# Causal grouped attention: the softmax division by block transposes on VectorE in place of two TensorE turns

## The reference, cut to what matters

```python
q = _rope((x @ Wq.T + bq) by head);  k = _rope((x @ Wk.T + bk) by head);  v = x @ Wv.T + bv
k, v = each repeated for 4 query heads
att = einsum('bhqd,bhkd->bhqk', q, k) / sqrt(16)
att = where(causal, att, -inf)
att = softmax(att, axis=-1)
y = einsum('bhqt,bhtd->bhqd', att, v)
return y.transpose(0, 2, 1, 3).reshape(b, t, n) @ Wo.T + bo
```

## Time and profile before

| | |
|---|---|
| time, median of 3 runs | 1556.51 us (1552.51 to 1558.87) |
| the profiled execution's own time | 1555.63 us |
| its span, from first to last instruction | 1553.9 us |
| mean granted clock of TensorE | 0.984 |
| busy share of the span: PE, DVE, ACT, POOL | 92%, 62%, 49%, 36% |
| the stage: its first DMA issue to that of the next stage | 1068.87 to 1227.92 us |

### The profile page before, as it was taken

One profiled execution on the slowest core, in us unless ns is written; L12 is line 12 of the kernel. 1 busy time (PEld: TensorE's weight loads), 2 busy tenths in 40 slices (PEclk: granted clock), 3 DMA queues, 4 the chain that ended last, 5 costly groups with the idle time before them and its releaser, 6 DMA issues. The chain is left out here.

```text
span 1553.9 us, 29211 instructions
## 1 busy us (share of the span) xinstructions
PE 1437.0 (92%) x10604; PEld 1116.8 (72%) x10630; DVE 968.4 (62%) x2214; ACT 754.9 (49%) x1878; POOL 562.0 (36%) x556
## 2 busy tenths in 40 slices
PE   6999999999899989899999999999899898999897
PEld 4778777787689777777777766896555688733586
DVE  5766667666565674756566566648675563677663
ACT  5565656656245334344343443453454353489352
POOL 2835619354136345525234200472000165110173
PEclk9999999999999999999999999999999899999998
DMA  3122231212282342303112005526000343222534
GB/s 144 59 90 69 85 103 42 90 63 90 69 330 79 112 148 103 115 17 103 40 45 99 1 1 214 201 97 227 9 2 2 131 140 129 64 63 47 188 100 139
DMA packets 57454, 149.48 MB, mean 96 GB/s; under 512 B 10225, under 2 KB 24689, under 8 KB 57201
## 3 DMA queue, kind: packets, MB, share of 16 engines
q1 hardware_dynamic: 39664, 89.58, 16.8%
q0 software_dynamic: 17664, 58.21, 11.0%
HBM read 104.77 MB, written 38.27 MB: 92 GB/s over the span
## 5 line engine op out<-in xcount | busy, mean ns | idle before, releaser
L145 POOL TENSOR_SCALAR ln_var<-ln_moments 128x4 f32<-128x4 f32 x16 | 4.0, 252 | 392.3 <-DVE ln_moments L130 242.4
L1376 ACT ACTIVATE s_scratch<-s_bank,s_neg_max 128x128 f32<-128x128 f32 (+3 forms) x128 | 67.2, 527 | 108.7 <-DVE s_neg_max L1467 108.5
L412 POOL DMA_INDIRECT expert_rows<-s_y,s_to_row x92 | 91.2, 991 | 57.8 <-ACT s_y L736 36.7
L1467 DVE TENSOR_REDUCE s_neg_max<-s_bank 128x1 f32<-128x128 f32 (+3 forms) x128 | 59.5, 487 | 52.5 <-PE s_bank L1262 52.2
L2811 POOL TENSOR_TENSOR s_w_hi<-s_w_raw,zero 128x1024 fp32r<-128x1024 f32 x25 | 55.5, 2221 | 100.0 <-PE s_memory L81 77.1
L1260 PE MATMUL s_bank<-s_k,s_q 128*128 128x128 f32 (+3 forms) x256 | 89.8, 446 | 0.0
L953 DVE TENSOR_TENSOR s_h_e<-s_bank,s_silu_e 128x176 f32<-128x176 f32 x92 | 31.4, 341 | 83.7 <-ACT s_silu_e L724 79.7
L79 PE MATMUL s_bank<-xn_t_hi,s_w_hi 128*128 128x512 f32 x192 | 79.7, 415 | 1.2 <-DVE xn_t_lo L212 1.2
L2476 ACT ACTIVATE s_exps<-s_bank,s_rms 128x512 f32<-128x512 f32 x128 | 76.4, 696 | 3.9 <-PE s_bank L2367 3.9
L1477 DVE TENSOR_SCALAR s_scratch<-s_scratch,s_row_sum 128x128 f32<-128x128 f32 (+3 forms) x128 | 75.4, 589 | 4.5
L405 POOL DMA_INDIRECT s_xg<-normed_rows,s_from_row x64 | 63.9, 998 | 38.5 <-DVE s_from_row L848 20.2
(11 more groups left out here) (429 smaller groups left out, 4852.5 us busy)
## 6 DMA issues: line engine op xcount, KB each, us to landing
s_expert_w_lo<-experts_lo SPq DMA_DIRECT2D x32, 608.0 KB, 13.1
s_e_lo<-in_experts POOLq DMA_DIRECT2D x32, 304.0 KB, 3.1
experts_hi<-s_e_hi POOLq DMA_DIRECT2D x32, 304.0 KB, 2.5
experts_lo<-s_e_lo POOLq DMA_DIRECT2D x32, 304.0 KB, 2.9
s_expert_w_hi<-experts_hi SPq DMA_DIRECT2D x16, 608.0 KB, 12.2
s_w_raw<-in_wa_o SPq DMA_DIRECT2D x16, 512.0 KB, 3.5
s_yg<-expert_rows SPq DMA_DIRECT2D x32, 256.0 KB, 4.5
s_raw<-in_shared SPq DMA_DIRECT2D x16, 384.0 KB, 6.4
```

The source lines that it names most:

```text
L412: pool.indirect_dma_start(out=y_rows[:, :], out_offset=bass.IndirectOffsetOnAxis(ap=to_row[:, i:i + 1].bitcast(U32), axis=0), in_=y[:, i % ...
L1376: act.activation(probs[:, h % 2, r, 0:(r + 1) * P], score_bank(h, r), ACT.Exp, bias=neg_max[:, 4 * h + r:4 * h + r + 1], accum_out=row_sum ...
L1467: dve.tensor_reduce(neg_max[:, 4 * h + r:4 * h + r + 1], score_bank(h, r), AX.X, ALU.max, negate=True).then_inc(max_done, 1)
```

## The change

The two TensorE turns and their two places in the ring are taken out. In their place VectorE divides in the layout that `o_raw` has: a block transpose of `o_raw` puts the sums of a slot on that slot's partitions by query (`by_query`), 16 reciprocals are taken, a second block transpose, whose source repeats each reciprocal 32 times, spreads them over the slot's rows (`inverse`, now 128 x 512), and a multiplication of two SBUF tiles gives `o`. The first transpose (`scale_o`) stands between M2a and M2b, the other three (`scale_rest`) between M1a and M1b, `low_o` behind `split_shift`, and `rotate_q` directly behind M3b. ScalarE's `high_o` reads SBUF and stands behind the last exponentials of the unit. In unit 7 the attended values are read from PSUM, without `copy_o`, and the matmuls of zeros between its attention and the last projection become 20 (they were 5 and 6).

```diff
-        o_raw, inverse, o = sb("o_raw", [P, S]), sb("inverse", [P, TB, KV_HEADS]), sb("o", [P, S])
+        o_raw, inverse, o = sb("o_raw", [P, S]), sb("inverse", [P, S]), sb("o", [P, S])
+        by_query, by_query_inverse = sb("by_query", [P, S]), sb("by_query_inverse", [P, S // SLOT])
...
                     if x == 1:
-                        order += [("turn", U - 1)] * (U > 0) + [("q", U + 2)] * (U + 2 < UNITS)
-                    if x == 3:
-                        order += [("back", U - 1)] * (U > 0)
+                        order += [("q", U + 2)] * (U + 2 < UNITS)
...
-            return order + [("turn", UNITS - 1), ("back", UNITS - 1), ("out", len(OUTS) - 1)]
+            return order + [("out", len(OUTS) - 1)]
...
-                    if j == 0:
-                        if U:
-                            turn_o(U - 1)
-                        if U + 2 < UNITS:
-                            project_q(U + 2)
-                    if j == 1 and U:
-                        turn_o_back(U - 1)
+                    if j == 0 and U + 2 < UNITS:
+                        project_q(U + 2)
...
-            turn_o(UNITS - 1)
-            turn_o_back(UNITS - 1)
-            keep_busy(pe, res, held("back", UNITS - 1)[:, 1, :], 6)
+            keep_busy(pe, res, held("att", UNITS - 1)[:, 1, :], 20)
             project_out(len(OUTS) - 1)
-            keep_busy(pe, res, held("back", UNITS - 1)[:, 1, :], 9)
+            keep_busy(pe, res, held("att", UNITS - 1)[:, 1, :], 9)
...
             def copy_o(U):
                 act.wait_ge(attended, TB * (U + 1))
                 if U:
-                    act.wait_ge(o_natural, U)
+                    act.wait_ge(o_scaled, U)
                 act.activation(o_raw[:], single("att", U), ACT.Copy).then_inc(o_copied, 1)

             def high_o(U):
-                act.wait_ge(o_ready, U + 1)
+                act.wait_ge(o_scaled, U + 1)
...
-                act.activation(o_hi[:, U % 3, :], single("back", U), ACT.Copy).then_inc(o_hi_done, 1)
+                act.activation(o_hi[:, U % 3, :], o[:], ACT.Copy).then_inc(o_hi_done, 1)
...
-                    if j == 1 and U:
+                    if j == (3 if U + 1 < UNITS else 1) and U:
                         high_o(U - 1)
...
-            copy_o(UNITS - 1)
             high_o(UNITS - 1)
...
             def scale_o(U):
-                by_head = single("turn", U).rearrange("p (t g s) -> p t g s", t=TB, s=SLOT)
-                dve.wait_ge(o_natural, U + 1)
-                dve.reciprocal(inverse[:], by_head[:, :, :, HD]).then_inc(inverse_done, 1)
+                if U + 1 < UNITS:
+                    dve.wait_ge(o_copied, U + 1)
+                    attended_values = o_raw[:]
+                else:
+                    dve.wait_ge(attended, TB * UNITS)
+                    attended_values = single("att", U)
+                if U:
+                    dve.wait_ge(sums_inverted, U)
+                dve.transpose(by_query[:], attended_values).then_inc(sums_turned, 1)
+
+            def scale_rest(U):
+                attended_values = o_raw[:] if U + 1 < UNITS else single("att", U)
+                dve.wait_ge(sums_turned, U + 1)
+                if U:
+                    dve.wait_ge(inverse_done, U)
+                dve.reciprocal(by_query_inverse[:], by_query[:].rearrange("p (b r) -> p b r", r=SLOT)[:, :, HD]).then_inc(sums_inverted, 1)
+                dve.wait_ge(sums_inverted, U + 1)
+                if U:
+                    dve.wait_ge(o_scaled, U)
+                dve.transpose(inverse[:], by_query_inverse[:].unsqueeze(2).broadcast_to([P, S // SLOT, SLOT])).then_inc(inverse_done, 1)
                 dve.wait_ge(inverse_done, U + 1)
                 if U:
-                    dve.wait_ge(o_ready, U)
-                dve.tensor_tensor(o[:].rearrange("p (t g s) -> p (t g) s", t=TB, s=SLOT),
-                                  single("turn", U).rearrange("p (t g s) -> p (t g) s", t=TB, s=SLOT),
-                                  spread(inverse[:].rearrange("p t g -> p (t g)"), SLOT), ALU.mult).then_inc(o_scaled, 1)
+                    dve.wait_ge(o_lo_done, U)
+                dve.tensor_tensor(o[:], inverse[:], attended_values, ALU.mult).then_inc(o_scaled, 1)
...
-                dve.tensor_tensor(o_lo[:, U % 3, :], single("back", U), f32(o_hi[:, U % 3, :]), ALU.subtract).then_inc(o_lo_done, 1)
+                dve.tensor_tensor(o_lo[:, U % 3, :], o[:], f32(o_hi[:, U % 3, :]), ALU.subtract).then_inc(o_lo_done, 1)
...
                 if ahead:
                     row_max(U + 1, 3, 0)
                     row_max(U + 1, 3, 1)
-                if U:
-                    scale_o(U - 1)
                 if U + 2 < UNITS:
                     rotate_q(U + 2)
                 if ahead:
                     row_max(U + 1, 2, 0)
+                if U:
+                    scale_o(U - 1)
+                if ahead:
                     row_max(U + 1, 2, 1)
                 if U + 2 < UNITS:
                     split_q(U + 2)
-                if U:
-                    low_o(U - 1)
                 if ahead:
                     row_max(U + 1, 1, 0)
+                if U:
+                    scale_rest(U - 1)
+                if ahead:
                     row_max(U + 1, 1, 1)
                     row_max(U + 1, 0, 0)
                     row_max(U + 1, 0, 1)
                     split_shift(U + 1)
+                if U:
+                    low_o(U - 1)
...
             scale_o(UNITS - 1)
+            scale_rest(UNITS - 1)
             low_o(UNITS - 1)
```

More of the change, by code:

```diff
@@ L1589, in causal_gqa_stage @@
         scores_ready, exp_done = sem("scores_ready"), sem("exp_done")
-        attended, o_copied, o_natural, inverse_done, o_scaled, o_ready, o_hi_done, o_lo_done = (
-            sem("attended"), sem("o_copied"), sem("o_natural"), sem("inverse_done"), sem("o_scaled"),
-            sem("o_ready"), sem("o_hi_done"), sem("o_lo_done"))
+        attended, o_copied, sums_turned, sums_inverted, inverse_done, o_scaled, o_hi_done, o_lo_done = (
+            sem("attended"), sem("o_copied"), sem("sums_turned"), sem("sums_inverted"), sem("inverse_done"),
+            sem("o_scaled"), sem("o_hi_done"), sem("o_lo_done"))
         out_ready, out_added = sem("out_ready"), sem("out_added")
@@ L1665, in read @@
                 return exp_done, scores_count(*at)
-            if kind in ("q", "shift", "att", "turn", "back"):
-                return {"q": q_rotated, "shift": q_shift_done, "att": o_copied, "turn": o_scaled, "back": o_lo_done}[kind], at[0] + 1
+            if kind in ("q", "shift", "att"):
+                return {"q": q_rotated, "shift": q_shift_done, "att": o_copied}[kind], at[0] + 1
             return out_added, at[0] + 1
@@ L1832, in attend @@
                 last.then_inc(attended, 1)
[L1834 to L1850, removed]
             def project_out(n):
```

## The result

The changed kernel takes 1569.23 us (median of 9 runs, 1563.72 to 1577.32), the kernel before 1558.66 in the runs beside it; the ratio is 1.0089, 95% interval 1.0065 to 1.0113. That is slower, by 13.9 us if the ratio is taken to 1558.66, where 8.2 over the profiled execution were forecast. 1569.23 lies above the forecast of 1563.8 and within its range of 1555 to 1570, the latter by luck: the range had left out the long spells, and long spells came. The forecast also held no measurable change (0.49) a little likelier than a loss (0.43). The profiled execution took 1566.87 us with a span of 1565.1.

The account below looks back on a forecast made before the run. No unit is simply full; the wait ending last at each ring step counts, with VectorE holding up TensorE at M1a. 1555.63 + 3.5 without the clock + 4.7 for clock falls = 1563.8 us, range 1555 to 1570.

Parts of the forecast that it names:

- long spells: Rival: clock spells in the units last longer, or the end's matmuls of zeros run slow; 1572 us and more, chance 0.06.
- the count and the length of the clock falls: Units 1 to 6: TensorE's clock falls in three of six, each spell 3.4 us and costing 1.6; +4.7 us.
- x7's wait: TensorE's step before attention waits for M1b behind VectorE's longer chain; start at 9.91 in place of 7.80, after 1.53 idle.
- The bound of 9.4 for six falls: Upper end of the clock term: one 3.4 us spell in each of units 1 to 6, 9.4 us lost.
- one or two (0.18): Case within falls in some units: only one or two of units 1 to 6 fall; chance 0.18, counted as same.
- The four instructions: VectorE's block transpose, reciprocal, block transpose and multiplication, priced at 0.71, 0.25, 0.71 and 0.69 us.
- the unit without the clock: Units 1 to 5 at the upper clock: 12.92 + 2.11 = 15.03 us, 0.68 more than 14.35.
- five units: Units 1 to 5 together, from VectorE's longer chain without clock loss: +3.4 us.
- Unit 6: Has neither `rotate_q` nor `split_q`, so its chain starts earlier; attention at 8.41 in place of 8.88, -0.5 us.
- the sum without the clock: Units 1 to 5, unit 6, unit 7 and the end: +3.4 - 0.5 + 0.6 + 0 = +3.5 us.
- The clock holds: Rival: TensorE's clock does not fall in the new gaps of units 1 to 6; 1559.1 us, chance 0.25.
- VectorE has room: Rival: VectorE's idle time absorbs the division, units 1 to 6 gain 1.43 us each; 1547, chance 0.08; half, 1555.6, chance 0.06.

Follow-up runs that it names:

- fill: The changed kernel with matmuls of zeros in TensorE's waits of units 1 to 6 (1, 2 and 6 ahead of x5, x6, x7); ratio to before 1.0018.
- fill_x5_x6: The changed kernel with matmuls of zeros ahead of x5 (1) and x6 (2) alone; ratio to the kernel before 1.0050.
- fill_x7: The changed kernel with six matmuls of zeros ahead of x7 alone; ratio to the kernel before 1.0022.
- all_behind: The changed kernel with first transpose directly behind M3b, reciprocal, second transpose and multiplication behind `split_shift`, `high_o` behind q_shift's copy; ratio to before 0.9986.
- delay_fill: The kernel before with three idle VectorE multiplications between M1a and M1b and matmuls of zeros in TensorE's waits, units 1 to 6; ratio 1.0055.
- best: all_behind with the reciprocal between M0a and M0b, `high_o` earlier where an output is due, unit 6's division in unit 6; 1542.67 us, ratio to before 0.9909.
- rest_behind: The changed kernel with reciprocal, second transpose and multiplication behind `split_shift`, `high_o` behind q_shift's copy, first transpose left in place; ratio to before 0.9985.
- before_delay: The kernel before with three idle VectorE multiplications of constants between M1a and M1b of units 1 to 6; ratio 1.0142.

## Why the prediction went as it did

**The step that failed** is the count and the length of the clock falls: "No row shows a gap exactly like this one, so I take three of six, between the ends: +4.7". It was six of six, five of them long, and 13.1 us. The stage's +15.72 divides by fill: 2.65 us stay when the waits are filled, 13.07 go with the clock, 2.2 for each of six falls. Two things in the step were off. I weighed one gap, x7's, and asked how often it alone would tip the clock; fill_x5_x6 shows that the answer to that question was nearly right, three of six at 1.7 us (16.61 against 14.98). But x5's and x6's waits, which I had priced at 0.35 and 0.47 us and used only for the share of busy time, make it a fall in every unit where x7's wait follows them, though by themselves they cost next to nothing (fill_x7, all executions). And together they make the fall come early, so that x7's wait lies inside the spell and the spell lasts 6.8 us: 17.21 - 14.89 = 2.32 lost, against 1.63 for a short one in fill_x5_x6. That the place of x7's wait makes the spell long is read from the traces: the five early falls of the changed kernel are long, while its late one in unit 6, and the early ones of fill_x7 with that wait filled, are short. The bound of 9.4 for six falls was therefore no bound, since it held the short length fixed, though the earlier trace rows had a long spell to show; I gave "long spells" 0.06. The chances of no fall (0.25) and of one or two (0.18) rest on the same step.

**What held.** The four instructions took 0.70, 0.24, 0.71 and 0.69 us, as priced. The chain on VectorE and what follows from it: x7 at 9.78 (9.91 forecast), the unit without the clock 14.89 (15.03), five units +2.8 (+3.4). Unit 6, counted to the first exponentials of unit 7, takes 15.96 us in fill and 16.18 before, 0.2 less (0.5 forecast); from there to the next stage's first DMA it is 21.61 against 21.49, 0.1 more (0.6). In all the sum without the clock was 3.5 and measured 2.65, 0.18% by the executions of fill (-0.03 to 0.40). `low_o` is hidden behind `split_shift`; the matmuls of zeros are free.

**The rivals.** "The clock holds" is what fill makes true, 2.8 us over the kernel before. "VectorE has room" was rightly refused for this order and rightly priced: all_behind gains 1.45 us in a plain unit against the 1.43 of unit 0, though only 0.2 in units 2 and 4. "Long spells" was the mechanism that came true.

The Trainium skill, "TensorE: Matmul & The Clock Gate", section "A second HAM failure mode: psum-queue depth-cycling", describes a kernel in which many small idle times between groups of matmuls, not one long one, make the clock swing between its two levels, and the loss lies in throughput. These runs agree in kind: with waits of 0.33, 0.59 and 1.59 us in a unit the clock swings in each of six, and with them filled it holds. They also show that short waits need not be enough: with 0.65 and 0.60 us the kernel before holds its clock.

## What to carry to other kernels

Where short waits of TensorE stand ahead of a long one, price a fall of its clock for the whole group, not for the longest wait alone, and price the long spell too. A trial with matmuls of zeros in the waits tells the clock's share from the chain's in one run, if they end before the wait does; in delay_fill they cost 0.27 us a unit themselves. Put new work of another engine behind the last instruction that TensorE's ring waits for: against a unit without a division (12.92), the same four instructions cost 1.97 us between the maxima, 0.54 more than the old division, and the clock took 2.3 on top; in all_behind, in VectorE's idle time and behind the maxima, they cost a plain unit nothing. Then look at who waits for the work's result: the edits of best at the tail of the stage gave 6.6 us in the profiled execution, the three plain units of all_behind 4.3 together.

## What the hardware showed that was not expected

- The clock fell in five of six units while TensorE was at work, ahead of its longest wait: at 1118.2 in unit 1, where the weight loads then stand idle from 1118.36 to 1119.95. A row of idle time beside a low clock is not the cause of it by standing there.
- All spells in units 1 to 6, in the profiled executions of all kernels, last about 3.4 or 6.8 us; the long ones occur there only with both groups of waits.
- The waits alone do not settle which unit falls: in rest_behind, units 1 and 3 have the same order and the same waits to 0.01 us (0.33 ahead of x5, 0.59 ahead of x6), and only unit 1 falls. What else decides stays open. One candidate is when in time the waits come. In the changed kernel the falls start 17.1, 20.5, 17.1, 20.5 and 17.1 us apart; in before_delay, whose units are 0.1 to 0.3 us longer, they start the same 17.1 and 20.5 us apart and so drift against the units, from 11.6 to 10.3 us behind the first maximum. In the changed kernel two units take 37.5 us, as two falls do, so six of six may owe something to that. No run shifted the waits in time.
